# Linear attention and a mixture of experts in one kernel: where the statistics are made, who rotates the values, and what the engines pass to each other in the attention steps

## The reference

```python
x = x + ln(attn(ln(x)))
x = x + ln(moe(ln(x)))

def attn(x):                       # 16 heads of 8 features, causal, linear
    q, k, v = split(x @ W_qkv + b_qkv)
    q, k = elu(q * 8 ** -0.5) + 1.0001, elu(k) + 1.0001
    for t in tokens:               # a running sum for each head
        kv += outer(k_t, v_t);  ks += k_t
        out_t = (q_t @ kv) / (q_t . ks + 1e-6)
    return out @ W_out + b_out

def moe(x):                        # 8 experts of 128-512-128 and a shared one
    g = top-2 of softmax(x @ Wr), rescaled to sum 1
    return ffn_shared(x) + sum over e of g_e * ffn_e(x)
```

## Time and profile before

| | us |
|---|---|
| median of 3 runs (lowest, highest) | 425.01 (423.76, 427.22) |
| the profiled execution | 424.23 |
| its span, first to last instruction | 422.5 |
| input and step 0 | 0 to 39.1 |
| step 1 | 39.1 to 64.9 |
| steps 2 to 6, as PE ends their output | 67.8 to 206.7 |
| step 7 | to 234.9 |
| passage, to the first second layer of a block | to 252.5 |
| blocks | to 380 |
| end | to 422.5 |

### The profile page before, as it was taken

How to read it: one execution, slowest core, us unless ns; L and a number is a source line. 1 busy time by engine, 2 the same in 40 slices (tenths; PEclk the granted TensorE clock), 3 DMA queues, 4 the chain that set the end, 5 groups by cost and what they waited for, 6 DMA issues and landing times.

```text
span 422.5 us, 9184 instructions
## 1 busy us (share of the span) xinstructions
PE 369.7 (88%) x2848; PEld 336.6 (80%) x2848; DVE 329.1 (78%) x907; ACT 240.7 (57%) x505; POOL 243.8 (58%) x318
## 2 busy tenths in 40 slices
PE   6689499889799797997977969999999999999970
PEld 3368479689598695985976969989999999997870
DVE  5899999999999999999899556866665555562292
ACT  3423354765856749468452667755666666653572
POOL 5510420585674865756637485777766666665282
PEclk9959889999999999999996989999999999999996
DMA  6999000010010000100101586999988888821953
GB/s 169 277 211 206 0 3 2 1 33 19 8 44 0 25 25 0 38 13 18 34 1 32 180 282 193 265 269 294 287 251 250 251 248 248 254 73 43 315 186 98
DMA packets 43772, 54.36 MB, mean 129 GB/s; under 512 B 4561, under 2 KB 34561, under 8 KB 43745
## 3 DMA queue, kind: packets, MB, share of 16 engines
q1 hardware_dynamic: 38906, 44.42, 37.9%
q0 software_dynamic: 4544, 9.35, 6.4%
q10 hardware_dynamic: 294, 0.26, 0.2%
HBM read 40.06 MB, written 18.15 MB: 138 GB/s over the span
## 4 chain that ended last, share of the span: by engine, by line
PE 51%; DVE 18%; ACT 12%; issue 7%; POOL 5%; DMA 4%; ACTq 1%; SPq 0%; POOLq 0%; DVEq 0%
PE bO L885 9%; PE bO L1080 8%; PE bS L1080 6%; DVE KV L1231 6%; ACT shared L570 3%; DVE KV L1225 3%; PE bV L849 3%; PE bA L868 2%; DMA expert_results<-yb,yrow 2%; PE bT L792 2%; PE bV L1057 2%; PE bV L1056 2%; PE bV L1055 2%; DVE bst L1154 2%; DVE Z L1241 2%
## 5 line engine op out<-in xcount | busy, mean ns | idle before, releaser
L533 POOL DMA_INDIRECT expert_results<-yb,yrow x78 | 83.8, 1074 | 35.7 <-issue 19.4
L491 POOL DMA_INDIRECT expert_lists<-rows,pos x64 | 78.3, 1223 | 22.0 <-issue 17.7
L1231 DVE TENSOR_TENSOR_SCAN KV<-bS,KV 128x1024 f32<-128x1024 bf16 x32 | 72.9, 2277 | 0.0
L885 PE MATMUL bO<-wout_rot,Z 128*128 128x128 f32 x512 | 63.3, 281 | 3.4 <-DVE Z L1241 2.5
L885 PEld LDWEIGHTS bO<-wout_rot,Z 128*128 128x128 f32 x512 | 61.6, 197 | 4.1 <-DVE Z L1241 2.8
L1545 DVE COPY yrow<-xb 128x2 int32<-128x2 int32 x39 | 9.4, 241 | 46.1 <-PE bO L1080 24.3
L452 POOL TENSOR_TENSOR ve<-mv,ln_eps 128x4 f32<-128x4 f32 x24 | 4.8, 200 | 69.9 <-DVE mv L1161 69.9
L1225 DVE SCALAR_TENSOR_TENSOR KV<-shared,bV 128x512 f32<-128x512 f32 x64 | 41.6, 671 | 2.0 <-PE bV L849 1.7
L849 PE MATMUL bV<-ident,shared 128*128 128x128 f32 x256 | 39.3, 290 | 3.2 <-ACT shared L608 2.6
L849 PEld LDWEIGHTS bV<-ident,shared 128*128 128x128 f32 x256 | 31.7, 152 | 6.3 <-issue 3.5
L868 PEld LDWEIGHTS bA<-w2s_sb,hs 128*128 128x128 f32 x256 | 31.8, 191 | 3.5 <-ACT hs L622 1.9
(11 more groups left out here) (318 smaller groups left out, 975.3 us busy)
## 6 DMA issues: line engine op xcount, KB each, us to landing
KV<-packed_weights SPq DMA_DIRECT2D x21, 578.0 KB, 4.7
Z<-packed_weights SPq DMA_DIRECT2D x18, 578.0 KB, 4.7
xb<-expert_lists SPq DMA_DIRECT2D x39, 129.0 KB
packed_weights<-in_L_ffn_Wfc SPq DMA_DIRECT2D x8, 256.0 KB, 9.6
packed_weights<-in_L_ffn_Wproj SPq DMA_DIRECT2D x8, 256.0 KB, 9.8
Z<-expert_results SPq DMA_DIRECT2D x4, 512.0 KB, 8.6
out<-SH SPq DMA_DIRECT2D x7, 256.0 KB, 2.3
KV<-expert_results SPq DMA_DIRECT2D x3, 512.0 KB, 6.1
```

The source lines that it names most:

```text
L491: g.indirect_dma_start(out=lists, out_offset=bass.IndirectOffsetOnAxis(ap=pos[:, m:m + 1], axis=0), in_=rows[:, m // TILES, m % TILES, :], ...
L533: g.indirect_dma_start(out=results, out_offset=bass.IndirectOffsetOnAxis(ap=yrow[n][:, c], axis=0), in_=yb[n][:, c, :], in_offset=None).th ...
L885: ins = t.matmul(bO[:, j * D:(j + 1) * D], Z[:, d, j * P:(j + 1) * P], wout_rot[:, d], start=False, stop=True, skip_group_check=True)
L1231: v.tensor_tensor_scan(w, ps_keep, w, 0.0, ALU.mult, ALU.add).then_inc(s["kv_sum"], 1)
```

## The change

- Input statistics leave the steps: DVE makes those of steps 0 to 3 ahead of the first step, ACT makes those of steps 4 to 7 by sums and squares with an accumulator (`late_sums` in front of iteration 0's work, `late_squares` at its end), POOL makes the roots in three goes.
- The residual's statistics: ACT's `attention_out` also sums what it writes, POOL forms the row sum of x1, and ACT squares x1 with an accumulator (`squares_of_x1`: four ACTIVATEs, between `rows_to_project` and `shared_out`). DVE's `sums_of(2)` and `mean_var(2)` go.
- Rotated v: v is one matmul without bias matmul; ACT adds the bias and writes it once (`v_rows`), and SP issues 14 DMAs a step from SBUF to SBUF (`rotate`). PE's 32 transposes a step go. k lies in PSUM (bank bV[0] as bK), and DVE multiplies two rotations at once, both from it.
- POOL also makes Z[0], `route_gaps`, `route_chosen`, `route_counts`, `route_placed`; ACT copies the logits. DVE converts no indices.
- Setup: the weights' copies go to ACT, the bias parts to POOL, the rotation of W_out behind the first projections.
- The packing of weights is spread between the rotations.
- The passage: ACT norms the attention's output ahead of the first block's weights; squares instead of DVE's statistics; the last second norm's transposes, logits and ranks come one block later; PE has 6 and 8 matmuls of zeros in iteration 7; POOL's last eight list scatters come after the results of blocks 0 and 1.

```diff
+            def rotate(st):
+                sp.wait_ge(s["v_ready"], st + 1)
+                for d in range(1, E):
+                    m = d * H
+                    sp.dma_start(vr[0:P - m, d], vr[m:P, 0]).then_inc(vr_in[d // 2], 16)
+                    sp.dma_start(vr[P - m:P, d], vr[0:m, 0]).then_inc(vr_in[d // 2], 16)
...
@@ POOL, iteration
                 if tail:
                     inv_std(1, i)
-                if nxt:
-                    inv_std(0, i + 2)
+                if nxt and routed:
+                    route_gaps(i)
+                    route_chosen(i)
                 if tail:
                     pool.wait_ge(s["attn_ready"], i)
+                    sum_of_x1(i)
                     g.tensor_tensor(Xs, Xs, attn[:], ALU.add).then_inc(s["x1_ready"], 1)
+                if nxt and routed:
+                    route_counts(i)
...
+                    g.tensor_tensor(Z[:, 0], KV[:, 0], qn[:], ALU.mult).then_inc(s["z0_ready"], 1)
                     g.tensor_tensor(Z[:, 1], KV[:, 1], qn[:], ALU.mult).then_inc(s["z1_ready"], 1)
+                if nxt and routed:
+                    route_placed(i)
+                if tail and nxt:
+                    inv_std2(i)
...
@@ ACT
+            def squares_of_x1(i):
+                act.wait_ge(s["x1_ready"], i)
+                alone(act)
+                for j in range(TILES):
+                    ins = a.activation(attn[:, j], Xt(i - 1, j), ACT.Square, scale=float(D),
+                                       bias=neg_sum2[:, j:j + 1], accum_out=sq2[:, j:j + 1])
+                ins.then_inc(s["sq_done"], 1)
...
-                a.activation(vdup[:, :, 0:D], v, ACT.Copy)
-                a.activation(vdup[:, :, D:2 * D], v, ACT.Copy).then_inc(s["vdup_ready"], 1)
+                a.activation(vr[:, 0], (bA if again else bH)[:], ACT.Identity, bias=bv_col).then_inc(s["v_ready"], 1)
+            def k_plus_eps(st):
+                act.wait_ge(s["k_read"], st + 1)
+                a.activation(r_qk[:, 1], r_qk[:, 1], ACT.Copy, bias=FEAT_EPS).then_inc(s["k_eps"], 1)
...
                 if nxt:
                     rows_to_project(i + 1, True)
+                if tail:
+                    squares_of_x1(i)
                 if routed:
                     shared_out(i - 2)
                     rows_of(i)
                 if nxt:
                     qk_maps(i + 1, True)
-                    v_twice(i + 1, True)
+                    v_rows(i + 1, True)
+                    k_plus_eps(i + 1)
...
@@ PE
                 if again:
                     pe.wait_ge(s["q_read"], st + 1)
-                add_bias(bank, 0)
-                for j in range(TILES):
-                    ins = t.matmul(bank[:, j * D:(j + 1) * D], xn_t[:, j * P:(j + 1) * P], w3[:, 2 * D:3 * D],
-                                   start=False, stop=True, skip_group_check=True)
+                    t.matmul(bA[:], w3[:, 2 * D:3 * D], xn_t[:], start=True, stop=True).then_inc(s["v_mm"], 1)
...
@@ PE, iteration: all v_rotated(...) and first_v(...) are gone
+                if not nxt:
+                    warm_up(8, bV[1])
                 out_part(i, 1)
...
@@ DVE
-            def prod(i, d):
+            def prod(i, pair):
...
-                dve.wait_ge(s["vt_done"], E * i + d + 1)
-                v.scalar_tensor_tensor(out=KV[:, d], in0=qk0[:, 1], scalar=FEAT_EPS, in1=bV[d % 2][:],
-                                       op0=ALU.add, op1=ALU.mult).then_inc(s["kv_prod"], 1)
+                dve.wait_ge(vr_in[pair], (64 if pair else 32) * (i + 1))
+                v.tensor_tensor(KV[:, 2 * pair:2 * pair + 2], bK[:].unsqueeze(1).broadcast_to([P, 2, STEP]),
+                                vr[:, 2 * pair:2 * pair + 2], ALU.mult).then_inc(s["kv_prod"], 1)
```

More of the change, by code:

```diff
@@ L271, in sandwich_kernel @@
         blk_scat = [sem(f"blk_scat{n}") for n in range(NBUF)]
+        x_in = [sem(f"x_in{n}") for n in range(2)]
+        vr_in = [sem(f"vr_in{n}") for n in range(E // 2)]
         y_in = [sem(f"y_in{n}") for n in range(NS)]
@@ L357, in _ @@
                          pads[:, NE:PADS, :, :].rearrange("p a c n -> p (a c) n")).then_inc(s["spare_in"], 16)
+            for e in range(0, NE, 2):
+                pack(e)
+                pack(e + 1)
+                rotate(2 + e // 2)
+            for st in range(2 + NE // 2, NS):
+                rotate(st)
             sp.wait_ge(s["spare_in"], 16)
@@ L473, in _, with bias_part_done @@
                    allow_small_or_imprecise_dtypes=True).then_inc(s["consts"], 1)
+            pool.wait_ge(s["rows_in"], 32)
+            parts = [0]
+            def bias_part_done(ins):
+                parts[0] += 1
+                ins.then_inc(s["bias_parts"], 1)
+                pool.wait_ge(s["bias_parts"], parts[0])
+            bias_part_done(g.tensor_copy(bias_f, bias_raw[:]))
+            for n in range(3):
+                row = slice(32 * n, 32 * n + 1)
+                bias_part_done(g.memset(ones3[row, :], 1.0))
+                bias_part_done(g.memset(eps3[row, :], bf16_parts(DEN_EPS)[n]))
+                bias_part_done(g.tensor_copy(bias_part[n][:], bias_f))
+                bias_part_done(g.tensor_copy(bias3[row], bias_part[n][row]))
+                if n < 2:
+                    bias_part_done(g.tensor_tensor(bias_f, bias_f, bias_part[n][:], ALU.subtract))
             def fill_pads():
@@ new lines, in setup_weights @@
+            def setup_weights():
+                act.wait_ge(s["setup_pe"], 3)
+                for half, bank in enumerate((bO, bV[1])):
+                    ins = a.activation(wout_rot[:, 4 * half:4 * half + 4],
+                                       bank[:].rearrange("p (a d) -> p a d", a=4), ACT.Copy)
+                ins.then_inc(s["setup_act"], 1)
+                act.wait_ge(s["w_rest"], 48)
+                a.activation(w1s_hi[:], w1s_sb[:], ACT.Copy).then_inc(s["w1s_hi"], 1)
+            act.wait_ge(s["w_first"], 32)
@@ L813, in project @@
                 t.matmul(bA[:], w3[:, 0:D], xn_t[:], start=True, stop=True).then_inc(s["q_mm"], 1)
+                if not again:
+                    t.matmul(bH[:], w3[:, 2 * D:3 * D], xn_t[:], start=True, stop=True).then_inc(s["v_mm"], 1)
                 if again:
@@ L983, in iteration @@
                     ins.then_inc(s["exp_done"], 1)
-                    v_rotated(i, 6, again)
                 if nxt:
@@ L1381, in iteration @@
                 again = from_on(i, 1)
+                alone_here = routed and not nxt
                 if isinstance(i, int) and i == 1:
```

499 lines of the change are left out of this document (299 added, 200 removed).

## The result

The changed kernel takes **413.94 us** (median of 4 runs, 412.34 to 414.61) where the kernel before takes 425.03 on the same chip (423.76 to 427.22): ratio 0.973, 95% interval 0.968 to 0.978. Its profiled execution took 414.61 with a span of 412.8. The prediction said 413.7. The time is right; the working behind it is right only in part, and its errors cancel. Marks of the same kind in both traces show it. "Out" is the matmul that ends a step's output, L919 before and L1133 after; step 7 ends with the logits, L898 and L1112.

The account below looks back on a forecast made before the run. The prediction took DVE to bound steps 0 and 1 and a ring of PE and ACT steps 2 to 6; -3.5 - 2.9 + 2.0 - 2.7 - 2.8 - 1.4 = -11.3 from 425.0 gave 413.7, range 402 to 426.

Parts of the forecast that it names:

- What bounds the loop: Steps 2 to 6: a ring of 27.7 us on PE and ACT is the limit, DVE's 27.3 just under it.
- The ring's terms: Steps 2 to 6: savings and additions on the PE and ACT ring sum to -0.1 us a step, before the clock.
- From v to out: Loop step: v, its bias matmul and first output matmuls replace copies and transposes of v, 1.5 us off the ring.
- -0.48 + 1.07 + 0.8: Loop step: four transposes before fc go (-0.48), squares of x1 add 1.07, eight accumulators add 0.8 (0 to 1.6).
- TensorE's clock, +0.5 a step: Loop: PE drops to 1.2 GHz in most steps, slowing v and first output matmuls, 0.5 us a step (0 to 2.5).
- the rival: Loop: clock falls every step and stays low through the output, 2.0 us more a step, 424 in all; chance 0.18.
- Start: Program start to end of step 0: earlier q and DVE's first products save 3.5 us (1 to 4.5).
- q about 3.3 us earlier: Step 0: q comes about 3.3 us earlier with W_out's rotation and three warm-up matmuls behind the projections.
- Step 1: Step 1, DVE busy throughout: it loses statistics, Z[0] and the product gain, -2.9 us.
- Step 7: Step 7: statistics gone, -1.2 us, and zeros keep PE's output matmuls at full rate, 1.5 less: -2.7.
- Passage, -2.8: Step 7's output to the second layers: DVE and attention_out no longer delay first blocks; lead 2.8 us from the third on.
- The stall at block 7, -1.4: Near block 7: DVE's wait for a result's scatter queued behind list scatters goes, saving PE about 1.4 us.

Follow-up runs that it names:

- e3: Changed kernel with eight unused BATCH_NORM_STATS added on DVE at the end of each of steps 2 to 6: 414.18 us, ratio 0.977.
- h1: Changed kernel with g3's edits; in steps 2 to 6 x1's statistics back on DVE, ACT's squares and attention accumulators gone: 407.58 us, ratio 0.960.
- e4: Kernel before, with six of eight BATCH_NORM_STATS of X and x1 left out in steps 2 to 6 (result not the reference's): 424.44 us, ratio 1.000.
- e1: Changed kernel with the shared result ahead of the squares of x1 on ACT: 431.97 us, ratio 1.020.
- g2: e1 with 12 matmuls of zeros on PE between k's and v's projection in steps 2 to 6: 420.23 us, ratio 0.993.
- e5: Changed kernel with 4 more matmuls of zeros on PE before the first projections: 448.23 us, kernel before 444.29 on that chip, ratio 1.011.
- e6: Changed kernel without the 14 matmuls of zeros in step 7: 451.72 us, kernel before 444.29 on that chip, ratio 1.013.
- g3: Changed kernel with 10 matmuls of zeros ahead of the second block's rows and the last second norm ahead of block 0's gelus: 413.23 us, ratio 0.975.
- e2: e1 with ACT's copies of the rows moved behind k + eps in steps 2 to 6: 420.89 us, ratio 0.992.
- g1: Changed kernel again, unedited, as a control on a third chip: 414.88 us, ratio 0.977.

## Why the prediction was right, and where it was not

- **What bounds the loop: right.** A ring of PE and ACT, DVE just under it. e3 shows it for the changed kernel, h1 from the other side; e4 agrees for the kernel before, less sharply.
- **The ring's terms: the sum was 0.4 off, and I know which.** From v to out: forecast -1.5, measured 10.14 (141.16 to 151.30) to 8.68, -1.46. From out round to the table load: forecast -0.48 + 1.07 + 0.8 = +1.4, measured 14.95 to 15.95, +1.0. The mis-sized term is the squares' ACTIVATE, priced by L570's row at 0.41 and measured at 0.29, so that the four with their sums fill the wait of 0.58 and put 0.95 on the ring, not 1.47; the price of 0.10 for an accumulator held (attention result 1.74 for 1.38). It has an immediate scale where L570 reads its scale from memory; whether that is the reason wasn't tried.
- **TensorE's clock, +0.5 a step: wrong for this order, right as a mechanism.** I put the new place (1.9 of work in 6 us) nearer to the stretch of the earlier trace rows that fell. It held at 1.00 in the four loop steps of the changed kernel, of its repeat and of e3. Only in step 2 of the changed kernel it stood at 0.50 for q and k (79.40 and 81.02, 1.82 and 1.91), which cost nothing, since v then followed without its wait. One order turned round (e1) made it fall in four steps of five, at up to 2.7 a step, and zeros (g2) brought it back; so it stood one edit away. That is why the rival had to be in the range.
- **Start: -3.5 was too much, -1.7 at DVE's mark.** The step that failed is "q about 3.3 us earlier" (12.34 before, 10.66 after). It started 1.7 earlier and ran at half rate, as did the transposes ahead of it. I moved PE's warm-up behind the projections in the text and didn't ask what the projections would then run at. The issues on SP took 0.60 each, not 0.42, six of them 1.1 more; e5 shows that they are what waits next.
- **Step 1: -2.9 came (-3.1 at DVE's mark) and 1.7 of both steps was given back.** By the end of step 1 PE's out lags DVE's Z by 4.5, 2.9 before: the PE ring takes over one step earlier, and DVE's lead has no user. These are readings of one profile each, good to about 1.
- **Step 7: right** (-2.9 for -2.7), and e6 confirms the 1.5 of the zeros.
- **Passage, -2.8: wrong, the lead came to +0.4.** I timed it from PE's output. What the first block waits for is DVE's table of blocks, for its weights, and the last of POOL's eight scatters of iteration 7, for its rows, and both follow DVE's and POOL's own work in iteration 7, not PE's output. DVE began the table 7.5 earlier (230.56, 223.09) and POOL the scatters 7.3 earlier (223.20, 215.88; they take 12.1 to 12.2 in both kernels), where the output came 8.9 earlier: the 1.5 that the zeros of step 7 win for PE's output is not won for them. The rows were issued 7.6 earlier (237.08, 229.47). That is 1.3 of it. g3 shows 0.4 to 0.9 as half rate and ACT's order. Some 1.0 isn't accounted for.
- **The stall at block 7, -1.4: gone and back.** The block there comes without the wait (-1.1 by the marks), and later ones lose 1.4 (second layers at 275.29, 282.66 two blocks on, then 286.67 and 290.43, for 3.42 a block). One of PE's two waits there (0.30 and 0.34) in the changed kernel:

```profile
284.95 0.44 PE L1244 MATMUL bT<-ident,xb 128*128 128x128 f32 x2 [0.34 <-DMA xb<-expert_lists]
```

While the lists are closed, SP issues a block every 3.9 us (before 3.8) for PE's 3.42. That the stall before had let SP catch up fits this, but wasn't tried; and in e3, with the same blocks, the stretch was 1.9 shorter than before, so that one profile doesn't decide whether the 1.4 is lost.
- **The sum:** -11.3 forecast, -9.7 in the span. Too hopeful by 3.3 at the start, by 3.2 in the passage and by 1.0 behind it, too gloomy by 5.0 in steps 2 to 6, and 0.7 at the end. The median is right by cancellation, which is luck. (The medians differ by 11.1; the profiled execution before was 0.8 under its median, the one after 0.7 over.) In the rotated values I had "no wait, under 1 us in hand", and named DVE waiting for vr as a sign of being wrong; DVE does wait for the second pair, 1.6 in step 2 and 0.7 in the later ones, inside its slack.

## What to carry to other kernels

When two limits stand almost on top of each other, price every moved instruction by the ring it lands on: this change took 3.7 us a step from the engine off the ring and put 1.9 (accumulators and squares, of which 0.6 filled a wait) on it, and undoing just that in five steps was worth more (some 6 us) than the loop had gained. Look at PE's longest wait in a step before reordering around it, and ask what each matmul that is moved away had kept busy. A forecast that hits the total should be checked stage by stage before it is believed.

## What the runs showed of the hardware

- An accumulator's read is a row of its own, 0.19 to 0.21 long, and adds 0.10 between ACTIVATEs in a row. The squares brought no third table load a step. The Trainium skill, ScalarE: Activation LUTs, Table sets, doesn't name Square among the functions of every set; the trace (two loads a step, as before) says that it behaves as one here.
- PE's clock fell behind an idle time of 2.82 (e6) and of 2.12 in the passage, and held behind 1.60 and 1.85 in one loop step. Behind 3.21 between two short bursts (e1) it fell in four steps and held in one, behind 2.06 and 2.07 (e2) it fell in one and held in four: no length of the idle time parts these cases.
- A product on DVE took 1.72 for 0.69 while POOL made one (e4), and in the changed kernel POOL's 128x4 product at 162.31 took 0.84 for 0.20 beside DVE's 128x1024 of Z. Work moved between the two meets the other there. The Trainium skill, SBUF — State Buffer, SBUF: two separate sides, has it that between a DVE instruction with two inputs in SBUF and one of GpSimd that reads SBUF, the one that starts later waits until the other's whole instruction is through; e4's rows agree: POOL's product had 1.17 to go when DVE's began.
- An issue of a DMA on SP took 0.51 to 0.63 from SBUF to SBUF (vr) and 0.42 to 0.43 for a load of weights from HBM.
- One of the chips ran the kernel before 20 us slower (444.29). Four variants of the changed kernel were 1.1 to 1.5% slower than it there, with pauses in which engines waited for something that the trace only calls remote, where the changed kernel is 2.7% faster in the result and 2.3% in g1. The kernel before has no trace from that chip.
